# Window attention on one core: scores once, with queries on partitions, and probabilities transposed by DMA

## The reference

```python
def layer(x):
    h = roll(_gn(x), (-3, -3))
    q, k, v = split(h @ w_qkv.T)                   # into windows: (B, heads, 64, 49, 32)
    dots = q @ k.T * 32 ** -0.5 + pos_emb[rel]     # 49 x 49 for each window and head
    dots += mask                                   # -inf across the seam, last row and last column of windows
    out = softmax(dots) @ v
    return x + roll(out @ w_out.T + b_out, (3, 3))
```

## Time and profile before

| | |
|---|---|
| median of three runs | 4584.58 us (4583.0 to 4586.03) |
| profiled execution | 4584.81 us |
| its span, first to last instruction | 4583.0 us |
| TensorE busy | 4390.2 us, 96% |
| VectorE busy | 4046.9 us, 88% |
| ScalarE and GpSimd busy | 2275.8 and 2282.0 us, 50% each |
| bytes moved by DMA | 478.93 MB |

### The profile page before, as it was taken

The page is one execution under the profiler, slowest core; times in us unless marked ns, Lnnn a source line. Parts: engine busy times, 40 slices in busy tenths (PEclk is TensorE's granted clock), DMA queues, the critical chain, the costliest instruction groups (busy, mean ns, idle before and its releaser), DMA issues.

```text
span 4583.0 us, 164167 instructions
## 1 busy us (share of the span) xinstructions
PE 4390.2 (96%) x64360; PEld 2981.1 (65%) x64360; DVE 4046.9 (88%) x9283; ACT 2275.8 (50%) x4225; POOL 2282.0 (50%) x1933
## 2 busy tenths in 40 slices
PE   3999999999999999999999999999999999999998
PEld 1666666666666666666666666666666666666665
DVE  5898898989989998898989989899898988999886
ACT  0555555455554545555555455555555555555554
POOL 1455445455554554555455455545545545554454
PEclk9999999999999999999999999999999999999999
DMA  4344344334343433443343443334434433434332
GB/s 122 103 106 107 99 107 116 94 108 114 99 109 105 108 104 103 107 109 98 105 119 95 108 112 100 107 106 108 105 97 109 115 95 107 115 98 108 98 95 60
DMA packets 231099, 478.93 MB, mean 105 GB/s; under 512 B 39009, under 2 KB 140898, under 8 KB 222818
## 3 DMA queue, kind: packets, MB, share of 16 engines
q1 hardware_dynamic: 230338, 468.43, 38.6%
HBM read 159.99 MB, written 77.07 MB: 52 GB/s over the span
## 4 chain that ended last, share of the span: by engine, by line
PE 74%; DVE 16%; issue 7%; ACT 2%; SPq 0%; DMA 0%; POOL 0%; DVEq 0%; POOLq 0%; ACTq 0%
PE ps_pj L1087 24%; PE ps_pj L1083 13%; PE ps_post L1181 13%; PE ps_post L1172 5%; PE ps_sa L1121 4%; PE ps_st L1121 3%; PE ps_pv L1165 2%; DVE mt L928 2%; PE ps_st L1150 2%; PE ps_pv L1164 2%; PE ps_pv L1163 2%; DVE atl L907 2%; DVE mw L917 2%; PE ps_pj L1071 2%; DVE st L701 1%
## 5 line engine op out<-in xcount | busy, mean ns | idle before, releaser
L554 POOL TENSOR_TENSOR pl<-pf,ph 64x588 f16<-64x588 f32 x512 | 732.1, 1430 | 1622.3 <-ACT ph L669 1595.0
L599 ACT ACTIVATE qk<-ps_pj 128x392 f16<-128x392 f32 x768 | 381.9, 497 | 978.7 <-PE ps_pj L1087 978.7
L669 ACT ACTIVATE ph<-ps_st,sc 64x588 f16<-64x588 f32 x1024 | 772.5, 754 | 6.5
L1087 PE MATMUL ps_pj<-xh,wh 128*128 128x392 f16 x2304 | 765.2, 332 | 5.5 <-POOL xl L529 4.6
L1087 PE MATMUL ps_pj<-xh,wl 128*128 128x392 f16 x2304 | 764.6, 332 | 0.0
L1087 PE MATMUL ps_pj<-xl,wh 128*128 128x392 f16 x2304 | 764.5, 332 | 0.0
L575 POOL TENSOR_TENSOR rb<-tq,cst 128x588 bf16<-128x588 bf16 x512 | 701.2, 1370 | 48.1 <-ACT tq L658 8.1
L529 POOL TENSOR_TENSOR xl<-xn,xh 128x392 f16<-128x392 f32 x384 | 343.4, 909 | 599.0 <-DVE vl L860 293.0
L865 DVE TENSOR_TENSOR qk<-ps_pj,qk 128x392 f16<-128x392 f32 x768 | 432.8, 564 | 228.3 <-ACT qk L599 225.4
L664 ACT ACTIVATE pf<-ps_st,sc 128x588 f32<-128x588 f32 x512 | 384.7, 751 | 359.1 <-PE ps_st L1121 359.1
L953 DVE TENSOR_TENSOR pl<-pf,ph 64x588 f16<-64x588 f32 x512 | 543.4, 1061 | 0.5 <-ACT ph L669 0.5
(11 more groups left out here) (107 smaller groups left out, 9582.0 us busy)
## 6 DMA issues: line engine op xcount, KB each, us to landing
stack<-qk SPq DMA_DIRECT2D x1536, 147.0 KB
sx<-in_x SPq DMA_DIRECT2D x66, 1176.0 KB, 7.0
xs<-in_x SPq DMA_DIRECT2D x384, 84.0 KB
out<-xb SPq DMA_DIRECT2D x384, 84.0 KB
xs<-in_x SPq DMA_DIRECT2D x384, 63.0 KB
out<-xb SPq DMA_DIRECT2D x384, 63.0 KB
xs<-in_x SPq DMA_DIRECT2D x128, 66.0 KB
out<-xb SPq DMA_DIRECT2D x128, 66.0 KB
```

What stands on the lines that cost most here:

```text
L554: nc.gpsimd.tensor_tensor(pl[PAD:, :, PAD:PAD + N], pf[PAD:, :, :], ph[PAD:, :, PAD:PAD + N], ALU.subtract).then_inc(s_pl[1], 1)
L669: e = nc.scalar.activation(ph[rows, :, w * PAD:w * PAD + N].rearrange("p (a h) n -> p a h n", a=2), ps_st[rows, :, 0:HH * N].rearrange("p ...
L1087: m = mm(ps_pj[bank][:, 0:RT].rearrange("p (w n) -> p w n", w=NW), wa[:, c, o:o + 128], xa[:, b, c, :, 0:N], **on)
```

## The change

Scores are computed once, with queries on partitions. Bias and mask come from four matmuls into the same bank, ahead of the scores (`bsel` picks the row of the table `bmov`). VectorE takes the maxima from PSUM (`maxima`) and subtracts them into the SBUF tile `lg` (`shifted`), ScalarE takes exp from `lg` in the same step (before: one step later), ph first. `pf`, `ph` and `pl` then have queries on partitions. SyncE transposes ph and pl by DMA into `pt`, 12 blocks of 128 x 128 each, in a new function `turn`. `pt` has two buffers; `ph`, `pl` and `lg` have one. The second set of scores, the shift rows and the work on the maxima are gone. The freed PSUM banks become a third bank for units and a bank of its own for the attended transposes.

```diff
+        pt = sb("pt", [128, 2, 2, HEADS, 2 * PAD], f16)
...
-        ps_st = ctx.enter_context(nc.psum_tensor("ps_st", [128, 2, 512], fp32))
+        ps_at = ctx.enter_context(nc.psum_tensor("ps_at", [128, 512], fp32))
-        ps_pj = [ctx.enter_context(nc.psum_tensor(f"ps_pj{i}", [128, 512], fp32)) for i in range(2)]
+        ps_pj = [ctx.enter_context(nc.psum_tensor(f"ps_pj{i}", [128, 512], fp32)) for i in range(BANKS)]
...
+                    turn(t)
                     if not (tk.first and k < 3):
                         store(t - 3, tk, k - 3)
+
+            def turn(t):
+                reach(s_pv, t - 1)
+                reach(s_ph, t + 1)
+                sp.dma_start_transpose(pt[:, t % 2, 0, :, :], ph[:, :, :].rearrange("p h n -> p (h n)")).then_inc(s_th, 16)
+                for w in range(2):
+                    reach(s_pl[w], t + 1)
+                sp.dma_start_transpose(pt[:, t % 2, 1, :, :], pl[:, :, :].rearrange("p h n -> p (h n)")).then_inc(s_tl, 16)
...

-                    pool.wait_ge(s_tc, t + 1)
-                    nc.gpsimd.tensor_tensor(
-                        rb[:, :, :, :], tq[:, :, :].unsqueeze(2).broadcast_to([128, 2, HH, N]),
-                        const_of("own_head").unsqueeze(1).unsqueeze(3).broadcast_to([128, 2, HH, N]),
-                        ALU.mult).then_inc(s_rb, 1)
+                    split_probabilities(t, n * 6 + 6 + sum(len(x_before(tk, i)) for i in range(min(k + 1, 4) if tk.last else k + 1)))
...

             def probabilities(t):
-                act.wait_ge(s_st, t + 1)
+                act.wait_ge(s_lg, t + 1)
+                need(act, s_th, 16 * t)
                 for w in range(2):
                     need(act, s_pl[w], t)
-                nc.scalar.activation(pf[:, :, :].rearrange("p (a h) n -> p a (h n)", a=2), ps_st[:, :, 0:HH * N], ACT.Exp,
-                                     scale=sc[:, 0:1])
-                need(act, s_pv, t)
                 for w in range(2):
                     rows = slice(w * PAD, (w + 1) * PAD)
+                    e = nc.scalar.activation(ph[rows, :, w * PAD:w * PAD + N], lg[rows, :, :], ACT.Exp, scale=sc[rows, 0:1])
                 e.then_inc(s_ph, 1)
+                nc.scalar.activation(pf[:, :, :], lg[:, :, :], ACT.Exp, scale=sc[:, 0:1]).then_inc(s_pf, 1)
...

+            def maxima(t):
+                dve.wait_ge(s_sa, t + 1)
+                nc.vector.tensor_reduce(mx[:, :].rearrange("p (a h) -> p a h", a=2), sa_out, AX.X, ALU.max).then_inc(s_mx, 1)
+
+            def shifted(t):
                 dve.wait_ge(s_mx, t + 1)
+                need(dve, s_pf, t)
+                nc.vector.tensor_tensor(lg[:, :, :].rearrange("p (a h) n -> p a h n", a=2), sa_out,
+                                        mx[:, :].rearrange("p (a h) -> p a h", a=2).unsqueeze(3).broadcast_to([128, 2, HH, N]),
+                                        ALU.subtract).then_inc(s_lg, 1)
...
             def split_probabilities(t):
-                dve.wait_ge(s_ph, t + 1)
-                need(dve, s_pv, t)
+                dve.wait_ge(s_pf, t + 1)
+                need(dve, s_tl, 16 * t)
...

+                for hh in range(2):
+                    for w in range(2):
+                        rows = slice(w * PAD, (w + 1) * PAD)
+                        mm(sa_out[rows, hh, :, :], bsel[:, kind, rows], bmov[:, :].unsqueeze(1).broadcast_to([128, HH, N]),
+                           start=True, stop=False, skip_group_check=True)
+                for h in range(HEADS):
+                    c, g = divmod(h, 4)
+                    for w in range(2):
+                        cols = slice((2 * p + w) * N, (2 * p + w + 1) * N)
+                        m = mm(sa_out[w * PAD:w * PAD + N, h // HH, h % HH, :], stack[0:96, odd, g, 1, c, cols],
+                               stack[0:96, odd, g, 0, c, cols], start=False, stop=True, skip_group_check=True)
...

-                for w in range(2):
-                    pe.wait_ge(s_pl[w], t + 1)
+                pe.wait_ge(s_th, 16 * (t + 1))
+                pe.wait_ge(s_tl, 16 * (t + 1))
```

More of the change, by code:

```diff
@@ L71, in constants @@
     low, right = tok // WS >= TALL, tok % WS >= TALL
-    for w in range(2):
-        t["flip"][N - 1 - tok, w * PAD + tok] = 1
-        t["eye"][w * PAD + tok, tok] = 1
-        t["window"][w * PAD:(w + 1) * PAD, w] = 1
+    rows_of = t["rows_of"].reshape(128, 4, 2, PAD)
+    row_masks = t["row_masks"].reshape(128, 4, 2, PAD)
     for at in BIAS_ROWS:
[L78 to L86, removed]
+        rows_of[at + N - 1 - tok, :, :, tok] = 1
     m = MASK_ROWS
+    for row, pattern in zip(m, (right, ~right, low, ~low)):
+        t["row_kinds"][row] = pattern
     for bottom in range(2):
@@ L569, in step @@
                         residual(t + 3, n, k + 3)
-                    if not (tk.first and k < 1):
-                        split_probabilities(t - 1, n * 6 + 6 + sum(len(x_before(tk, i)) for i in range(min(k + 1, 4) if tk.last else k + 1)))
-                        pool.wait_ge(s_pl[1], t)
-                    pool.wait_ge(s_tc, t + 1)
-                    nc.gpsimd.tensor_tensor(
-                        rb[:, :, :, :], tq[:, :, :].unsqueeze(2).broadcast_to([128, 2, HH, N]),
-                        const_of("own_head").unsqueeze(1).unsqueeze(3).broadcast_to([128, 2, HH, N]),
-                        ALU.mult).then_inc(s_rb, 1)
+                    split_probabilities(t, n * 6 + 6 + sum(len(x_before(tk, i)) for i in range(min(k + 1, 4) if tk.last else k + 1)))
             def image(m):
@@ L642, in step @@
                         x_highs(tk, k)
+                    probabilities(t)
+                    if not (tk.last and k >= 4):
                         units(tk, k, 1)
-                    if not (tk.first and k < 1):
-                        probabilities(t - 1)
-                    shift_rows(t)
-                    if not (tk.last and k >= 4):
                         units(tk, k, 2)
@@ L971, in step @@
                     t = 8 * n + k
-                    logits(t, tk, k)
-                    maxima(t, k)
-                    if not (tk.last and k >= 4):
-                        units(tk, k, 0)
-                    if not (tk.first and k < 3):
-                        attended_low(t - 3)
+                    maxima(t)
+                    shifted(t)
+                    between(5)
                     if tk.finishes and k == 4:
@@ L980, in step @@
                         stat_sums()
-                    maxima_by_window(t, k)
+                    if not (tk.first and k < 3):
+                        attended_low(t - 3)
+                    if not (tk.last and k >= 4):
+                        units(tk, k, 0)
                     between(5)
-                    maxima_high(t)
-                    between(5)
-                    maxima_low(t)
                     if not (tk.first and k < 2):
@@ L1000, in step @@
                     between(5)
[L1001 to L1002 removed]
+                    split_probabilities(t)
                     if not (tk.last and k >= 4):
```

244 lines of the change are left out of this document (71 added, 173 removed).

## The result

The changed kernel takes 5771.07 us (median of 4, 5760.09 to 5773.05) against 4583.80: ratio 1.258, interval 1.256 to 1.261. It is slower by 26%; 5320 us, 16% slower, was forecast.

A forecast was written before the change was run, and what follows sets the result against it. SyncE's DMA queue was taken to bound the changed kernel at 10.13 us a step: 110.5 + 511 x 10.13 + 27.9 = 5315 us, plus 1.8 around it and some 4 for the last transposes, 5320 us; range 4280 to 8750.

The forecast's parts named there:

- The mechanism: SyncE's queue, which issues every DMA in program order, sets the pace at 10.13 us a step; chance 0.50.
- TensorE busy for 78%: Sign of being right: TensorE busy for some 78%, waiting at attention for the landed low part.
- Where the stall goes: The low part lands late, attention waits on TensorE, and maxima wait for the logits buffer, ph and pl.
- the queue's sum: SyncE in four steps: 24.1 us of present DMAs plus 8 x 2.05 for transposes, 40.5 us against TensorE's 31.4.
- 2.05 us an issue: SyncE's price for issuing one transpose, the longest stack copy issue, between 0.6 us and 7.2 us.
- TensorE's step: TensorE's work a step: 8.40 less 1.04 removed plus 0.5 for four bias matmuls, 7.86 us.
- The third bank: With the separate bank for attended transposes, removes TensorE's waits for VectorE: at most 0.30 us a step, at least nothing.
- VectorE: VectorE loses 1.30 us a step of window product and maxima parts, from 7.8 to 6.5; busy near 65%.
- The data: DMA engines carry eight transposes, 3.15 MB, in 12.9 us beside the present 13.6, within four steps of 31.4 us.
- the packet bound: Rival: each 256-byte row segment is a packet of 70 ns on the DMA engines; 16.85 us a step, 8750 us; chance 0.07.
- The landing cycle: Rival: single buffer pl, GpSimd's 1.43 + issue 0.6 + landing 7.0 = 9.03 us a step, 4760 us; 0.06 together with bursts.
- The cheap-issue rival: SyncE issues a transpose in 0.6 to 0.76 us, deciding below 1.34; 8.1 us a step, 4285 us; chance 0.28.

The follow-up runs named there:

- The small kernel: Nothing but DMAs: transposes of 128 x 1536, 128 x 768 and 128 x 128, plain copies, and transposes beside row loads; no version of the kernel; 241.12 us.
- the 687 us: From the changed kernel without transposes after two steps, 4299.6 us, to plain copies instead of transposes with two buffers each for ph and pl, 4986.4 us.

## Why the prediction was right

- **The mechanism** held: SyncE's queue, two thirds full before, is what ends last. The step is 11.03 us for 10.13, and the kernel is slower by 26% where the forecast says 16%: the sign and the bound were right, the size was short by 451 us.
- **TensorE busy for 78%**, as forecast, is luck. The forecast is 7.86 / 10.13; the profile has 4495.3 us of 5770, more than the 4390.2 before the change, where the kernel without transposes has 3968.5. The number of matmuls is the same in both; a q or k matmul lasts 353 to 361 ns for 332, at a mean granted clock of 0.90.
- **Where the stall goes** was wrong. "Attention waits on TensorE" for the landed low part: the trace has 5 us of that in all. TensorE stands 602 us at the output projection for atl, and exp waits 1407 us for the landed high part. Between the two lie 1312 us in which VectorE, which makes atl, waits for q and k units that ScalarE copies behind exp; how much of the 602 comes that way is argued from the program, not shown.
- **The term that was mis-sized** is the queue's sum. 8 issues at 2.05 were taken, 8 at 1.88 came (1.4 us less), and these were not in the sum: 2.4 us of waits in program order, 1.1 for the waits of `turn` themselves, 1.5 of gaps. Together they are the 3.6 us from 40.5 to 44.1. The prediction let the queue be either full or free; it is 94% full and waits in between. Start and end came near: 107.5 and 29.1 us for 110.5 and 31.9.
- **2.05 us an issue** was near by luck. It is the middle between ends twelve times apart, and the upper end has the twelve blocks worked through one after the other. The small kernel shows 1.10 us for one block and 1.43 for twelve, and above it the pace of the DMA engines; of the mean of 1.88, then, some 0.45 is the hold-up, and half of that stands behind the slab, a load that the prediction does not reckon with.
- **TensorE's step** of 7.86 us: without transposes it is 8.17 with 0.46 of standing for atl, so at most 7.7 of work. The bias matmuls took 0.38 for 0.5. The third bank was worth 0.15 us of the 0 to 0.30 given.
- **VectorE** was to fall to 6.5 us a step and has 3248.4 / 512 = 6.3; that the share is 56% and not 65% is the longer step.
- **The data**: 12.9 us for eight transposes was the sum's number; at 1.83 each they take 14.6 alone, and the share of 0.73 over 44.1 us is 32 us with the rest. The 70 ns for each 256-byte piece, the packet bound, were far off: 1.83 us x 16 / 1536 is 19 ns.
- **The landing cycle** exists, with 3.75 us and not 7.0, and on ph rather than pl. With the one on pl it costs 174 us and not the whole difference.
- **The cheap-issue rival** was priced wrong. Had the issue been short, this step of the prediction would have failed. "It decides below 1.34 us" is not so: plain copies cost the queue 0.55 us, and the kernel took 5261, not 4285 (whose terms add up to 4283). The sum of a queue was taken for its time. Its waits inside a fixed order, the single buffer and the lateness of whatever stands behind a new wait were named in the text and then given a few tenths.
- **Open**: how the 687 us divide between bytes and order; the order is on the path, its share is not measured.

No version here that keeps all of the transposition beats the kernel before. Less data alone (half of each transpose) is not enough at 5062.

## What to carry to other kernels

A queue that only issues DMAs has a budget like an engine: add up its issues for a cycle of steps, then add the waits that stand in its program order, and ask of every new wait which transfers queue behind it. A transpose by DMA cost the queue more than two plain copies even at one block (1.10 us against 0.47), and the engines twice a plain copy's time. Moving the loads to another queue did not help here, it cost 166 us. A large load ahead of such an issue makes it long: look at what stands before the longest ones. A kernel with everything but the transposes, measured first (4300 us here), shows what one may pay for them.

## What the runs showed of the hardware

- A DMA transpose of two-byte elements held SyncE for 1.10 us (128 x 128), 1.21 (128 x 768) and 1.43 (128 x 1536) with nothing else under way, a plain copy of 393 KB for 0.47.
- With the DMA share near 1 the issue grew: 1.83 us each in a row, up to 8.37 beside another queue's loads, 3.18 and 3.75 in the mean behind a slab of 1.18 MB.
- Issue to landing in a row was 2.3 us for one block, 2.8 for six, 4.2 for twelve at the median.
- The mean granted clock of TensorE fell from 0.998 to 0.90 in the changed kernel, with 0.76 in the stretch shown; its q and k matmuls took 353 to 361 ns for 332. TensorE is on 2% of the chain.
